# Layer 1's attention result kept once in f32 and projected by f32 products, with the work of the steps placed anew

## The chip, the core and the metric

The kernel runs on one core of a Trainium2 chip. The metric is the device time of one execution, in microseconds (us), as the median of three. A core has a matrix engine (TensorE, PE in the rows; PEld is its weight load), a vector engine (VectorE, DVE), a scalar engine (ScalarE, ACT), GpSimd (POOL), a queue engine that issues transfers (SyncE, SP) and 16 DMA engines. Each engine runs its own instructions in the order in which they are written, and the engines wait for one another by semaphores only.

## The reference, cut to what matters

Two conditioned transformer blocks act on `x` (2 x 1024 x 288), in f32. Both have 16 heads of 18 values. Block 0 is ordinary attention over tokens with an MLP behind it. In block 1 the attention runs inside a token, from head to head:

```python
# layer 1: n = 2, t = 1024, d = 288, H = 16, DH = 18
q, k, v = (qkv[:, :, 0], qkv[:, :, 1], qkv[:, :, 2])      # n t H DH
attn = jnp.einsum('nthd,ntkd->nthk', q * scale, k)        # 16 x 16 scores for each token
attn = jax.nn.softmax(attn, axis=-1)
out = jnp.einsum('nthk,ntkd->nthd', attn, v)
out = out.transpose(0, 2, 1, 3).reshape(n, t, d)          # heads first, then tokens
return out @ proj_w + proj_b
...
x = x + gate_msa[:, None, :] * _attention(...)
x = x + gate_mlp[:, None, :] * _mlp(_modulate(_layernorm(x), shift_mlp, scale_mlp), ...)
```

The `transpose` puts heads ahead of tokens before the reshape, so a row of 288 that is projected holds 16 tokens of one head. No projected tile of batch entry 0 exists before half of all steps are done, and none of entry 1 before the last step.

## The kernel before

**Precision.** Most products take a number as two f16 parts, high and low, and add the products high x high, low x high and high x low. An f32 operand goes to TensorE as it is; the trace shows two matmul records for each f32 matmul that the code issues.

**Layer 1's attention** is `head_attention`, written once for each engine. Its tokens are cut into 4 pieces of 512 (`NPIECE`), each piece into 4 steps of 128 tokens, so there are 16 steps (`NSTEP`). A step's 128 tokens make 16 "cells" of 128 x 32 numbers side by side in one PSUM bank of 128 x 512. For each step k:

- `cell_scores(k)` (PE, L1602): 16 f32 matmuls from `q_rows` and `k_ring`.
- `subtract_maxima(k)` (DVE, L1141 and L1144), `exponents_of_cells(k)` (ACT, L1379), `invert_sums(k)` (DVE, L1151 and L1154), `scale_cells(k)` (POOL, L795 and L799), `turn_cells(k)` (DVE, L1162).
- `widen(k)`: two quarters by POOL (L811), two by ACT (L1334), into `p_wide`, of which there is one buffer.
- `cell_values(k)` (PE, L1620): 16 f32 matmuls from `p_wide` and `v_cells`, into bank 6 or 7.
- `high_attention(k)` (ACT, L1384) copies the bank as f16 into `attn`; `low_attention(k)` (DVE, L1177) subtracts that from the bank and stores the rest as f16.

The loops run these staggered. In step k, PE issues the scores of k + 1 and the values of k - 2; DVE issues turn_cells(k - 2), invert_sums(k - 1), subtract_maxima(k) and, from k = 3, low_attention(k - 3); POOL issues widen(k - 2) and behind it scale_cells(k - 1).

**What else runs in the steps** is set by tables of step numbers that all engines read:

- `ROWS_AT`: `rows_mms(i, m)` (PE, L1633) makes the m-th of 7 row pieces of q, k and v of token piece i, in 7 f16 matmuls of 512 columns. `take_rows` (ACT, L1355) copies it out and stores it to `qkv_rows` in DRAM.
- SP fetches it from there: `fetch_q(i)`, `fetch_k(k)` (three buffers) and `fetch_v(i)`, which waits until all four turns of the piece before are done (`v_turned`).
- `TURN_V_AT`: `turn_v(i, a)` (DVE, L1170), four for each piece. The first step of a piece can't weigh its values before all four.
- `TILES_AT`: `normalise` and `low_part` (DVE, L936, L940 and L946) of token tiles 12 to 15, `turn` (PE, L1579) two steps later.
- `JOB_STEPS`: the MLP's weights are cut into parts: `high_weights` (ACT, L1341) one step early, `low_weights` (DVE, L1021) in the step, the next raw load (SP) two steps later. There is one raw buffer, `w_raw`.
- `OUT_AT`: `out_mms(t)` (PE, L1651) projects tile t of batch entry 0 into bank 2 or 3; `take_projection` (DVE, L1056), `add_projection` (POOL, L781) and `mid_statistics` (DVE, L926 to L931) one step later.

Behind the steps the eight tiles of batch entry 1 are projected, four, then the turns of four MLP tiles, then four. The first chunk of the MLP follows on PE (L1848).

**The projection's weights.** `attn` puts head h's value d at partition 32a + d of block r, so the 288 weight rows lie in four blocks of 128 partitions with gaps. `head_rows_job` loads them in two jobs, gaps filled with zeros; DVE splits them into `proj_high` and `proj_low` (L999 and L1008) in layer 0's last MLP chunk.

## Time and profile before

| | |
|---|---|
| time, median of 3 | 892.95 us (891.84 to 893.7) |
| the profiled execution's own time | 893.41 us |
| its span | 891.4 us |
| busy, share of the span | PE 88%, DVE 72%, ACT 59%, POOL 32% |
| layer 1's attention, from the first cell_scores to the first L1848 | 641.0 to 766.6 us |
| projections of batch entry 1 | 750.7 to 766.6 us |

The profiled execution is 0.46 us above the median. Times in the rows are from the start of the span. A busy PE is not PE at its peak, since its matmuls overlap. Where each number is read stands below, in the groups of rows.

### The profile page before, as it was taken

The page shows a single profiled execution, that of the slowest core. Times are in us where ns is not written, and L with a number is a line of the kernel's source. Part 1 is how long each engine was busy: PE and PEld are TensorE (multiplying, and loading weights), DVE is VectorE, ACT ScalarE, POOL GpSimd, SP SyncE. Part 2 cuts the span into 40 slices and gives each one's busy share as a digit, 9 for nine tenths or more (in the row PEclk, how much of TensorE's full clock was granted, in tenths as well). Part 3 has the DMA queues.
Part 4 walks back from the last instruction along what each step waited for, and adds up shares of the span by engine and source line. Part 5 has one row for each costly group of instructions (what it writes and reads, how often), then busy time and mean ns, then how long its engine had stood idle before and what let it go on. Part 6 is the DMA issues. An engine that isn't in the chain of part 4 may idle for free.

```text
span 891.4 us, 16501 instructions
## 1 busy us (share of the span) xinstructions
PE 781.1 (88%) x6096; PEld 363.8 (41%) x6096; DVE 643.1 (72%) x1277; ACT 525.9 (59%) x731; POOL 281.8 (32%) x369
## 2 busy tenths in 40 slices
PE   1569889999988989899898999999979986999996
PEld 0235222222221222222234465566646654566555
DVE  4849888898887898888936955746688897764531
ACT  4433577777776677777785725635547734634640
POOL 4311011325554241102023337241223565342122
PEclk9979799999999999999999999999989996999998
DMA  7302011110111110000040011101676730000000
GB/s 221 83 22 74 21 29 28 28 48 12 41 43 50 45 28 21 21 22 21 2 110 2 11 41 42 22 18 49 155 178 161 175 66 28 8 28 1 26 26 27
DMA packets 52127, 45.35 MB, mean 51 GB/s; under 512 B 23898, under 2 KB 41236, under 8 KB 52055
## 3 DMA queue, kind: packets, MB, share of 16 engines
q1 hardware_dynamic: 47613, 36.35, 15.9%
q10 hardware_dynamic: 4442, 8.04, 2.8%
q8 instruction: 45, 0.74, 0.4%
q14 instruction: 27, 0.22, 0.1%
HBM read 27.66 MB, written 9.46 MB: 42 GB/s over the span
## 4 chain that ended last, share of the span: by engine, by line
PE 55%; DVE 25%; ACT 5%; issue 4%; POOL 4%; DMA 3%; SPq 2%; ACTq 1%; DVEq 0%; POOLq 0%
PE ps L1869 12%; DVE row_max L966 12%; PE ps L1734 10%; PE ps L1695 8%; PE ps L1848 6%; PE ps L1633 4%; PE ps L1686 4%; PE ps L1722 3%; DVE mlp_area L1107 2%; SPq L579 2%; PE ps L1651 2%; PE ps L1602 1%; DVE probs L936 1%; DVE probs L940 1%; ACT mlp_area L1499 1%
## 5 line engine op out<-in xcount | busy, mean ns | idle before, releaser
L966 DVE TENSOR_REDUCE row_max<-ps 128x1 f32<-128x512 f32 x512 | 321.0, 684 | 55.3 <-PE ps L1695 54.2
L1458 ACT ACTIVATE probs<-ps 128x1024 f32<-128x1024 f32 x256 | 249.1, 1018 | 56.9 <-PE ps L1722 56.2
L1695 PE MATMUL ps<-stack_area 54*128 54x512 f16 x512 | 144.6, 390 | 28.3 <-DVE row_max L966 21.2
L1734 PE MATMUL ps<-probs,mlp_area 128*32 128x512 f32 x1024 | 137.2, 608 | 0.0
L1722 PE MATMUL ps<-stack_area 56*128 56x512 f16 x512 | 111.0, 385 | 7.2 <-ACT probs L1458 7.2
L1869 PE MATMUL ps<-w_fc,mlp_area 128*128 128x288 f16 x864 | 109.4, 289 | 4.7 <-DVE mlp_area L1107 4.7
L1695 PEld LDWEIGHTS ps<-stack_area 54*128 54x128 f16 x512 | 35.6, 93 | 187.2 <-DVE row_max L966 173.5
L1848 PE MATMUL ps<-mlp_area,w_fc 128*128 128x512 f16 x504 | 110.8, 379 | 0.8 <-ACT mlp_area L1499 0.8
L1499 ACT ACTIVATE mlp_area<-ps 128x512 f32<-128x512 f32 x72 | 42.9, 595 | 97.9 <-PE ps L1848 95.4
L1869 PEld LDWEIGHTS ps<-w_fc,mlp_area 128*128 128x128 f16 x864 | 84.6, 99 | 28.3 <-DVE mlp_area L1107 3.9
L769 POOL TENSOR_SCALAR neg_scaled<-neg_max 128x16 f32<-128x16 f32 x16 | 4.1, 254 | 271.2 <-DVE neg_max L973 271.2
L1848 PEld LDWEIGHTS ps<-mlp_area,w_fc 128*128 128x128 f16 x504 | 48.6, 98 | 60.7 <-ACT mlp_area L1499 4.3
L1120 DVE SCALAR_TENSOR_TENSOR probs<-ps,fc_bias 128x288 f32<-128x288 f32 x32 | 14.6, 457 | 78.1 <-PE ps L1869 78.1
L879 POOL TENSOR_TENSOR probs<-probs,ada (+2 forms) x32 | 26.1, 814 | 141.0 <-DVE probs L1120 140.7
L1107 DVE SCALAR_TENSOR_TENSOR mlp_area<-mlp_area 128x512 f16<-128x512 f32 x72 | 49.9, 701 | 17.7 <-ACT mlp_area L1503 17.5
L1503 ACT ACTIVATE mlp_area<-mlp_area 128x512 f16<-128x512 f32 x72 | 45.4, 630 | 2.7
L1722 PEld LDWEIGHTS ps<-stack_area 56*128 56x128 f16 x512 | 29.7, 94 | 36.5 <-ACT probs L1458 14.8
L1686 PE MATMUL ps<-tokens 128*126 128x512 f16 (+1 forms) x140 | 43.7, 441 | 0.0
L940 DVE SCALAR_TENSOR_TENSOR probs<-probs,rstd,ada 128x288 f32<-128x288 f32 x64 | 36.3, 567 | 8.0 <-DVE probs L936 0.9
L936 DVE SCALAR_TENSOR_TENSOR probs<-x_sb,mean_var,ada 128x288 f32<-128x288 f32 x64 | 37.0, 579 | 2.0 <-DMA ada<-ada_rows 1.0
L1579 PE MATMUL ps<-ident,probs 128*128 128x128 f16 x96 | 12.3, 270 | 28.4 <-DVE probs L946 21.8
L1633 PE MATMUL ps<-mlp_area,w_qkv 128*126 128x512 f16 (+1 forms) x147 | 35.3, 395 | 0.8 <-ACT mlp_area L1373 0.8
(170 smaller groups left out, 1082.1 us busy)
## 6 DMA issues: line engine op xcount, KB each, us to landing
stack_area<-tokens SPq DMA_DIRECT2D x124, 36.0 KB
qkv_rows<-part_area ACTq DMA_DIRECT2D x14, 252.0 KB
qkv_rows<-probs ACTq DMA_DIRECT2D x10, 252.0 KB
x_sb<-in_x SPq DMA_DIRECT2D x4, 576.0 KB, 7.6
w_raw<-in_L_cond_W_fc SPq DMA_DIRECT2D x4, 576.0 KB
tokens<-qkv_rows SPq DMA_DIRECT2D x64, 36.0 KB
v_sb<-qkv_rows SPq DMA_DIRECT2D x16, 144.0 KB
w_raw<-in_L_cond_fc_w SPq DMA_DIRECT2D x4, 576.0 KB
```

Of the source, the lines that this page charges most:

```text
L936: nc.vector.scalar_tensor_tensor(xn[u], x_sb[:, t, :], mean_var[:, t, 0:1], ada[:, b, s + 1, :], ALU.subtract, ALU.mult).then_inc(xn_done[ ...
L966: nc.vector.reduce_max(row_max[:, p % 2, t, j, half:half + 1], bank(bk), AX.X).then_inc(max_done, 1)
L1107: nc.vector.scalar_tensor_tensor(gs[:, f, 1, :], g_sb[f % 2], HS, gs[:, f, 0, :], ALU.mult, ALU.subtract).then_inc(g_split, 1)
L1458: nc.scalar.activation(probs[:, n % 2, 2 * c:2 * c + 2, :].rearrange("p h n -> p (h n)"), ps[:, 2 + 2 * c:4 + 2 * c, :].rearrange("p b n - ...
L1499: nc.scalar.activation(g_sb[f % 2], bank(2 + f % 2), gelus[l], scale=UN).then_inc(g_ready, 1)
L1633: mm = nc.tensor.matmul(bank(2 + n % 2)[0:end - first, :], w_qkv[:, w, first:end], piece_columns(i)[:, a, :], start=(x == 0), stop=(x == l ...
L1686: mm = nc.tensor.matmul(bank(bk)[0:rows], w_qk[:, w, row:row + rows], hT_all[:, a, t0:t0 + 512], start=(i == 0), stop=(i == len(PRODUCTS) ...
L1695: nc.tensor.matmul(bank(bk), stacks[rows, p % RING, 0, t * P:(t + 1) * P], stacks[rows, p % RING, 1, half * 512:(half + 1) * 512], start=T ...
L1722: mm = nc.tensor.matmul(bank(2 + 2 * c + j), stacks[rows, p % RING, 1, n * P:(n + 1) * P], stacks[rows, p % RING, 0, c * 512:(c + 1) * 512 ...
L1734: mm = nc.tensor.matmul(bank(6)[at:at + VW, :], v_pad[:, TB * (p // BPAIR) + n, 2 * (p % BPAIR) + j, :], probs[:, n % 2, 2 * c + j, :], st ...
L1848: mm = nc.tensor.matmul(bank(2 + f % 2), w_fc1[:, w, f * P:(f + 1) * P], h2T[:, a, :], start=(i == 0), stop=(i == len(PRODUCTS) - 1))
L1869: mm = nc.tensor.matmul(bank(4 + i % 2)[:, 0:C], gs[:, f, a, i * P:(i + 1) * P], w_fc2[:, w, f, :], start=(f == 0 and (a, w) == (0, 0)), s ...
```

## The change

It touches layer 1's attention alone.

- `high_attention` and `low_attention` become one copy by ACT, `take_attention`, that leaves the bank in f32. The 16 DVE subtractions are gone. PE's `cell_values` waits for the copy (`a_taken`) in place of the subtraction (`a_low`).
- The projection's weights are kept as f32 in four blocks, `proj_rows`. POOL clears them (four memsets in layer 0's second MLP chunk), SP loads 16 pieces of 18 rows and the bias straight into place (`load_heads`). The two split jobs on DVE and their raw loads are gone.
- `out_mms` issues 4 f32 matmuls of 288 columns where it issued 12 of f16.
- The tables of step numbers are new, and in a step ACT takes rows ahead of `high_weights`, widens ahead of the attention copy, and DVE splits weights ahead of `normalise`, the statistics and `take_projection`.

```diff
-        attn = [free2[:, 8192 * (1 - b):8192 * (2 - b)].bitcast(F16).rearrange("p (s r n) -> p s r n", s=2, r=4)
+        attn = [free2[:, 8192 * (1 - b):8192 * (2 - b)].bitcast(F32).rearrange("p (r n) -> p r n", r=4)
                 for b in range(B)]
-        proj_high = [w_proj_area[:, 0:2 * C], free4[:, 4608:4608 + C].bitcast(F16)]
-        proj_low = [w_proj_area[:, 2 * C:4 * C], free_v[:, 4224:4224 + C].bitcast(F16)]
+        proj_rows = [w_proj_area[:, 0:2 * C].bitcast(F32), w_proj_area[:, 2 * C:4 * C].bitcast(F32),
+                     free4[:, 4608:4608 + C], free_v[:, 4224:4224 + C]]
...
-        JOB_STEPS = {2: 5, 7: 6, 12: 7, 17: 8}
+        JOB_STEPS = {1: 3, 7: 4, 12: 5, 16: 6}
...
-        JOBS_AT_FC2 = {0: (0, 2), 3: (0, 2)}
+        JOBS_AT_FC2 = {0: (0, 2)}
...
-        TILES_AT = {2: (12, 13), 3: (14, 15)}
-        ROWS_AT = {0: [(1, 3), (1, 4)], 1: [(1, 5), (1, 6)]}
...
+        TILES_AT = {1: (12,), 2: (13, 14), 4: (15,)}
...
-        OUT_AT = {11: (0, 1), 12: (2, 3), 13: (4, 5), 14: (6,), 15: (7,)}
...
+        OUT_AT = {11: (0, 1, 2), 12: (3,), 13: (4, 5), 14: (6,), 15: (7,)}
...
+            def load_heads():
+
+                sp.wait_ge(heads_cleared, len(proj_rows))
+                rows = proj_w[1].rearrange("(r a d) n -> r a d n", r=4, a=4)
+                for r, dst in enumerate(proj_rows):
+                    for a in range(4):
+                        sp.dma_start(dst[HC * a:HC * a + D, :], rows[r, a]).then_inc(heads_in, 16)
+                sp.dma_start(proj_rows[0][D:D + 1, :], proj_b[1].rearrange("(r n) -> r n", r=1)).then_inc(heads_in, 16)
...
-            load_weights(1, QKV_JOBS, HEAD_JOBS)
+            load_heads()
...
-            def low_attention(k):
-
-                b, dst = k // 8, attn_cells(k // 8, 1, k)
-                dve.wait_ge(a_high, k + 1)
-                nc.vector.tensor_tensor(dst, bank(6 + k % 2).rearrange("p (x t g) -> p x t g", t=2, g=4), attn_cells(b, 0, k),
-                                        ALU.subtract).then_inc(a_low, 1)
...
-            def high_attention(k):
+            def take_attention(k):
 
                 act.wait_ge(ev_mm, k + 1)
-                nc.scalar.activation(attn_cells(k // 8, 0, k), bank(6 + k % 2).rearrange("p (x t g) -> p x t g", t=2, g=4), ACT.Copy
-                                     ).then_inc(a_high, 1)
+                nc.scalar.activation(attn_cells(k // 8, k), bank(6 + k % 2).rearrange("p (x t g) -> p x t g", t=2, g=4), ACT.Copy
+                                     ).then_inc(a_taken, 1)
...
                 if k > 1:
-                    pe.wait_ge(a_low, k - 1)
+                    pe.wait_ge(a_taken, k - 1)
...
-                steps = [(r, s, part) for r in range(4) for s, part in ((0, proj_high), (1, proj_high), (0, proj_low))]
-                for x, (r, s, part) in enumerate(steps):
-                    mm = nc.tensor.matmul(bank(2 + t % 2)[:, 0:C], attn[b][:, s, r, cols],
-                                          part[r // 2][:, C * (r % 2):C * (r % 2 + 1)],
-                                          start=(x == 0), stop=(x == len(steps) - 1))
+                for r in range(4):
+                    mm = nc.tensor.matmul(bank(2 + t % 2)[:, 0:C], attn[b][:, r, cols], proj_rows[r],
+                                          start=(r == 0), stop=(r == 3))
```

The rest of the tables, as piece and number by step: the row pieces were (1,3) (1,4) in step 0, (1,5) (1,6) in 1, three of piece 2 in step 3 and two each in 4 and 5, three of piece 3 in step 6 and two each in 7 and 8. They are (1,3) to (1,6) in step 0, three of piece 2 in step 2, two in 3, one in 5 and one in 6, of piece 3 one in step 6, four in 7, one each in 8 and 9. The turns of v were four in step 0, then two each in 3, 4, 8, 9, 12 and 13; they are four in step 2, one each in 4 and 5, two each in 6, 8, 9, 12 and 13.

What stands in a row on DVE in steps 1 and 2, first before. L1151 opens invert_sums, L1141 subtract_maxima, L1162 is turn_cells, L1021 the weight split, L936 and L940 a tile's normalise.

```order
L1170 STREAM_TRANSPOSE v_sb<-v_sb 128x512 [waits v_in] x4
L1151 TENSOR_REDUCE v_sb<-probs 128x32 [waits cell_exp]
L1154 RECIPROCAL v_sb<-v_sb 128x32 [waits cell_total]
L1141 TENSOR_REDUCE v_sb<-ps 128x32 [waits cell_sub,cell_mm]
L1144 TENSOR_TENSOR part_area<-ps,v_sb 128x512 [waits cell_top]
L1162 STREAM_TRANSPOSE stack_area<-probs 128x512 [waits cell_done]
L1151 TENSOR_REDUCE v_sb<-part_area 128x32 [waits cell_exp]
```

The same place in the changed kernel (L1143, L1133, L1154 and L1013 are these lines there, L928 and L932 normalise, L938 low_part, L1162 turn_v):

```order
L1136 TENSOR_TENSOR part_area<-ps,v_sb 128x512 [waits cell_top]
L1013 SCALAR_TENSOR_TENSOR w_fc<-w_raw,w_fc 128x1152 [waits late_high]
L928 SCALAR_TENSOR_TENSOR probs<-x_sb,mean_var,ada 128x288
L932 SCALAR_TENSOR_TENSOR probs<-probs,rstd,ada 128x288 [waits xn_done0,rstd_ready]
L1154 STREAM_TRANSPOSE stack_area<-probs 128x512 [waits cell_done]
L1143 TENSOR_REDUCE v_sb<-part_area 128x32 [waits cell_exp]
L1146 RECIPROCAL v_sb<-v_sb 128x32 [waits cell_total]
L1133 TENSOR_REDUCE v_sb<-ps 128x32 [waits cell_sub,cell_mm]
L1136 TENSOR_TENSOR probs<-ps,v_sb 128x512 [waits cell_top]
L938 TENSOR_TENSOR probs<-probs 128x288 [waits hi_ready0]
```

Two normalise pairs and the four turns of v follow there, as the last work of step 2; before, the turns were the last of step 0. The split of the weights and a normalise moved ahead of the first turn_cells.

PE in step 11 before, with two projections ahead of the scores of step 12:

```order
L1651 MATMUL ps<-w_proj,mlp_area 128x288 [waits a_low,rows_taken,w_ready]
L1651 MATMUL ps<-w_proj,mlp_area 128x288 x5
L1651 MATMUL ps<-stack_area,mlp_area 128x288 x2
L1651 MATMUL ps<-v_sb,mlp_area 128x288
L1651 MATMUL ps<-stack_area,mlp_area 128x288 x2
L1651 MATMUL ps<-v_sb,mlp_area 128x288
```

And in the changed kernel, where the third tile's first matmul waits for DVE to have taken the first (`proj_y`), and the scores (L1585) stand behind it:

```order
L1633 MATMUL ps<-w_proj,mlp_area 128x288 [waits a_taken,rows_taken,heads_in]
L1633 MATMUL ps<-w_proj,mlp_area 128x288
L1633 MATMUL ps<-stack_area,mlp_area 128x288
L1633 MATMUL ps<-v_sb,mlp_area 128x288
L1633 MATMUL ps<-w_proj,mlp_area 128x288 [waits rows_taken]
L1633 MATMUL ps<-w_proj,mlp_area 128x288
L1633 MATMUL ps<-stack_area,mlp_area 128x288
L1633 MATMUL ps<-v_sb,mlp_area 128x288
L1633 MATMUL ps<-w_proj,mlp_area 128x288 [waits proj_y]
```

A tile went from 12 matmuls to 4, and three tiles stand in step 11 instead of two.

## Rows read from the trace of the kernel before

**Rows 1.** Two stretches: us; busy us (records) of PE, PEld, DVE, ACT, POOL; clock; DMA

```profile
680.00:700.00 20.00, 20.00 (x249) 12.82 (x246) 12.93 (x21) 14.73 (x24) 7.29 (x13) 1.00 0.68 169
720.00:740.00 20.00, 15.28 (x264) 10.56 (x255) 19.61 (x37) 6.98 (x12) 14.21 (x21) 1.00 0.12 33
```

**Rows 2.** The chain that ended last, 749 to 767 us: start, us, what

```profile
749.23 0.61 ACT mlp_area L1384
749.86 0.70 DVE mlp_area L1177
750.70 8.17 PE ps L1651 x48
...
760.76 5.99 PE ps L1651 x48
```

**Rows 3.** A stretch of the first four projections, TensorE alone: busy, clock

```profile
752.00:754.00 2.00, 2.00 (x10) 0.50 0.00 0
```

**Rows 4.** f32 on TensorE by line: ns min/median/max, first and last start, shapes

```profile
L1744 PE MATMUL ps<-w_fc,silu_t x24: 406/406/431, 63.1 to 64.4; 96*32 96x288 f32 x24
L1710 PEld LDWEIGHTS ps<-ident,w_qkv x64: 138/140/144, 124.2 to 477.0; 128*128 128x128 f32 x64
```

**Rows 5.** TensorE in order of time: start, us, line, shapes [idle before, releaser]

```profile
122.92 1.06 PE L1734 MATMUL ps<-probs,mlp_area 128*32 128x512 f32 x8
...
661.12 1.95 PE L1602 MATMUL ps<-tokens,stack_area 128*32 128x128 f32 x32 [3.22 <-DMA tokens<-qkv_rows]
662.99 6.38 PE L1633 MATMUL ps<-mlp_area,w_qkv 128*126 128x512 f16 x21
...
685.87 4.75 PE L1633 MATMUL ps<-mlp_area,w_qkv 128*126 128x512 f16 x21
```

**Rows 6.** VectorE in step 15, in order of time: start, us, line

```profile
736.64 0.70 DVE L1162 STREAM_TRANSPOSE stack_area<-part_area 128x512 f32<-128x512 f32 x1
...
739.49 0.45 DVE L1056 SCALAR_TENSOR_TENSOR probs<-ps,ada 128x288 f32<-128x288 f32 x1
739.85 0.68 DVE L1177 TENSOR_TENSOR mlp_area<-ps,mlp_area 128x512 f16<-128x512 f32 x1
740.45 0.70 DVE L1162 STREAM_TRANSPOSE stack_area<-probs 128x512 f32<-128x512 f32 x1
```

**Rows 7.** VectorE: the L1162 that open steps 11, 12, 13, 14, 17, and two statistics

```profile
710.27 0.71 DVE L1162 STREAM_TRANSPOSE stack_area<-part_area 128x512 f32<-128x512 f32 x1
...
714.47 0.70 DVE L1162 STREAM_TRANSPOSE stack_area<-probs 128x512 f32<-128x512 f32 x1
...
717.32 0.45 DVE L926 BATCH_NORM_STATS2 bn<-x_sb 128x6 f32<-128x288 f32 x1
...
718.10 0.45 DVE L926 BATCH_NORM_STATS2 bn<-x_sb 128x6 f32<-128x288 f32 x1
...
725.08 0.66 DVE L1162 STREAM_TRANSPOSE stack_area<-part_area 128x512 f32<-128x512 f32 x1
...
732.86 0.68 DVE L1162 STREAM_TRANSPOSE stack_area<-probs 128x512 f32<-128x512 f32 x1
...
744.10 0.71 DVE L1162 STREAM_TRANSPOSE stack_area<-part_area 128x512 f32<-128x512 f32 x1 [1.45 <-POOL part_area L799]
```

**Rows 8.** GpSimd in order of time: the widen of step 10, the last widen

```profile
707.44 1.27 POOL L811 COPY stack_area<-stack_area 32x512 f32<-32x512 f32 x2 [1.04 <-DVE stack_area L1162]
...
744.87 2.31 POOL L811 COPY stack_area<-stack_area 32x512 f32<-32x512 f32 x2 [0.81 <-DVE stack_area L1162]
```

**Rows 9.** ScalarE's first high_weights of the steps

```profile
652.29 1.16 ACT L1341 ACTIVATE w_fc<-w_raw 128x1152 f16<-128x1152 f32 x1 [0.86 <-DMA w_raw<-in_L_cond_fc_w]
```

**Rows 10.** VectorE: the first four turns of v, a normalise, the first weight split

```profile
644.60 3.93 DVE L1170 STREAM_TRANSPOSE v_sb<-v_sb 128x512 f32<-128x512 f32 x4 [0.20 <-DMA v_sb<-qkv_rows]
...
655.40 0.51 DVE L936 SCALAR_TENSOR_TENSOR probs<-x_sb,mean_var,ada 128x288 f32<-128x288 f32 x1
...
656.46 1.35 DVE L1021 SCALAR_TENSOR_TENSOR w_fc<-w_raw,w_fc 128x1152 f16<-128x1152 f32 x1
```

74 lines of the change are left out of this document (29 added, 45 removed).

## Prediction

> **What bounds the kernel now.** I read the stretches first, to see which engine is full where the change acts [rows 1], then the chain of waits behind the steps [rows 2], then each engine in order of time inside the steps [rows 5 to 8]. There are three parts. From about 662 to 703 us TensorE is full (20.00 of 20 us) and the vector engine is not (12.93): the row pieces fill it. From about 703 to 741 us it is the other way round, DVE 19.61 of 20 and PE 15.28. From 747 us on the chain of waits shows what is last [rows 2]: last values, ACT's copy, DVE's subtraction, and then TensorE without a gap through eight projections and four turns to the MLP at 766.6 us. So a vector instruction saved counts in the second part only, and a TensorE instruction added counts in the first and third.
>
> **The product, priced.** Four f16 projections take 5.99 us in 48 matmuls [rows 2], 1.50 us a tile. No row shows an f32 matmul of 128 rows and 128 weight columns that isn't a transpose. The nearest are of 32 weight columns, four side by side. Eight of 512 columns take 1.06 us [rows 5]: two groups, so at most 0.53 us for 512 columns and 0.30 for 288, with the last one's tail in it. The 24 of 288 columns start within 1.3 us [rows 4], six groups, five steps, 0.26. As an estimate, 0.24 to 0.26 us a record, two records for each matmul issued, eight a tile: 1.95 us. That is 0.45 us more than now, for every one of the 16 tiles. The bounds: 1.9 (0.24) and 2.1 (0.26); 0.30 holds a tail that a stream hides. A 128-column f32 weight load takes 0.138 us [rows 4], and lies under a 0.24 us matmul if it overlaps as the f16 loads do.
>
> **Last part: eight tiles.** 8 x 0.45 = +3.6 us (bounds 3.2 and 4.8), all on the path, since TensorE has no gap there. The first four tiles took 8.17 us where the others took 5.99, at half the clock [rows 2, 3], a loss of 2.2. TensorE idles between the last value products as before, so I keep this loss; it can come out 1 less or 1.5 more, for a slower stream that starts at another moment.
>
> **First part: the start.** The early row pieces move ahead. TensorE idled 3.22 us before the scores at 661.12, waiting for a fetch [rows 5]; three pieces in step 2 can fill that. But the turns of v of piece 0 moved from step 0 to the end of step 2, and the first values wait for them. The vector engine can't come there early: `low_weights` now stands in step 1, and its `high_weights` can't begin before the raw weights land at 652.3 and takes 1.16 [rows 9]. From 653.5 on DVE has in a row: split 1.3 [rows 10], a normalise 1.06 (656.46 - 655.40 [rows 10]), one step of turn, sums and maxima 2.85 (739.49 - 736.64 [rows 6]), a low part of some 0.4, two normalises 2.1, four turns 3.9 [rows 10]. That ends near 665.1. Until then TensorE can do the scores of step 3 and three row pieces; then it idles some 3 us. By the same moment the kernel before had done 0.7 of a piece, one step's scores (1.75) and one step's values (1.0) more: the change is 2.3 pieces of 1.58 us (4.75 / 3 [rows 5]) ahead and 2.75 behind, 0.9 ahead. In step 4, which has no row piece, ACT's two column copies stand ahead of its widen, and the values wait about 1.1 us. The clock fell before in the like idle time (21 row matmuls took 6.38 us where 21 others took 4.75 [rows 5]), and some 0.6 us of that loss came behind 665; I take 0.8. Sum at the values of step 9: -0.9 + 1.1 + 0.2 = +0.4. Bounds -3 (the 3.22 us of idle filled at no price) and +3 (it comes back in full). `fetch_v(1)` now waits for the turns, and holds fetch_k(6), fetch_k(7) and a weight load behind it on SP's queue; I expect them in time, by some 3 us.
>
> **Second part: steps 9 to 13.** Each low_attention takes 0.60 us to the next instruction [rows 6]. But a step has a second limit. turn_cells, widen (1.27), mask, scale and their waits go round between DVE and GpSimd: from the widen's start at 707.44 to the next turn at 710.27 is 2.83, with the turn ahead and its wait (0.74) 3.57 [rows 7, 8]. A bare step with the subtraction takes 3.8 (740.45 - 736.64, with a take) [rows 6]. So bare steps gain 0.25, not 0.60. In detail: steps 9 and 10 give 0.8 by the start of step 11 (710.3 to 709.5), where TensorE arrives last. Step 11 took 4.20 [rows 7]. Now three tiles stand ahead of the scores: 3 x 1.95 from 709.5 is 715.4, and the take of the third and the next turn come at 716.0: 6.5 us. Step 12 took 10.61 [rows 7]; less 0.60, less one take 0.36 [rows 6], plus one statistic 0.78 [rows 7], less some waits, 10.3. Step 13 took 7.78; less 0.60, less one statistic: 6.4. Step 14 begins at 709.5 + 6.5 + 10.3 + 6.4 = 732.7, now 732.86: -0.2. The projections of this part thus eat the vector engine's gain, mostly in step 11.
>
> **Steps 14 to 17 and the last values.** Now 732.86 to 744.10, 11.24 us [rows 7]. By the round trip 3 x 3.57 = 10.7. The last weight split moves from step 17 to 16. Beside it GpSimd's last widen took 2.31 us for 1.27 [rows 8]; now this 1.04 falls on step 16's widen or scale, and no longer on the last widen. So the turn of step 17 comes at 732.7 + 10.7 + 1.0 = 744.4, +0.3; the widen behind it gives back 1.04, and the subtraction that goes, 749.86 to 750.70, gives 0.84 [rows 2]. The first projection starts at 750.7 + 0.3 - 1.0 - 0.8 = 749.2, -1.5 to -1.7.
>
> The row shows a loss of 1.04 beside a split of 1.3. The Trainium skill (SBUF — State Buffer, the part on the shared port pair) says that VectorE with two SBUF inputs and GpSimd exclude each other for a whole instruction. By it the price could be the split's full length, 1.3, in step 16, and the total 0.3 higher than by the row.
>
> **At no price.** The two split jobs in layer 0's last chunk: DVE waits there for row pieces and ACT anyway. POOL's four memsets of 288 columns: GpSimd, busy 32% of the span, waits for DVE behind them in that chunk; without that cover, each would cost what a copy of 512 columns does, 0.6 us [rows 8]. `load_heads` issues 17 transfers early, for 18 in two bursts. ACT's copy keeps its length; only the output's type differs.
>
> **Sum.** Start of the last projections -1.6, eight tiles +3.6, clock 0: +2.0 us. On the profiled execution's 893.4 this is 895.4; it stands 0.46 above the median of the runs, so 892.95 + 2.0 = 895.0.
>
> **The rivals.**
> 1. *The vector engine's gain carries (faster).* If TensorE reaches step 11 early enough that the third projection doesn't hold the scores, and the start keeps its lead, ten subtractions in steps 9 to 18 come off in full, 6.0 us. Then 892.95 - 6.0 + 3.6 = 890.5. For it: TensorE was busy 15.28 of 20 us there [rows 1], and the eight tiles add only 3.6. Against: the round trip of 3.57, and three tiles in a row. It decides from 2.5 us of lead at step 11.
> 2. *Gain and price balance.* The early pieces keep 2 us of their lead, nothing else differs: 893.0.
> 3. *The clock.* Half clock for two more tiles' length in the last part, or a second fall in step 2 or 4: +2 to +3, 897.5. For it: new idle near 662 and 675 us. A page speaks for it too: the Trainium skill (TensorE: Matmul & The Clock Gate, on loop structure) warns that idle gaps halve the clock.
> 4. *Weight loads don't overlap.* Each f32 record would cost 0.24 + 0.138 [rows 4], 64 of them in the last part +8.8, more in the steps: 904. Against it: at 0.125 us an f16 record hides a load of 0.10. The Trainium skill (TensorE: Matmul & The Clock Gate, the mechanism of packing) states that loads overlap a running matmul only if the row group differs. By that rule this rival is what happens; the f16 rows speak against it.
> 5. *The change doesn't do what it says:* the spread row pieces win nothing since the values wait for the turns of v. That is in my forecast.
>
> **How the numbers follow.** Forecast 0.45 (its own range 893.6 to 897), rival 1 0.22, rival 2 0.20, rival 3 0.09, rival 4 0.04. A measurement of this kernel tells about 0.2%, 1.8 us, from no change. The forecast lies just beyond that, so some 0.1 of its 0.45 falls within; rival 2 lies within. Faster 0.23, same 0.31, slower 0.46. The range for 8 in 10 runs from rival 1's 890.5, its far side left out, to 898.3 in rival 3.
>
> **What would show it.** Right: the f32 projection at about 0.24 us a record; the last part, first projection to first L1848's like, at 19 to 20 us against 15.9; the first values near 665 us, released by DVE's turns of v; in step 11 the vector engine waiting 2 us for projections; the last projections starting near 749. Wrong: a start of the last part before 747 (rival 1), a tile of 3 us (rival 4), TensorE's clock at half for over 5 us in the last part (rival 3).

## The result, and the profile after

The changed kernel takes 896.0 us (median of 9 runs, 894.6 to 897.1), the kernel before 892.6 (9 runs beside it). The ratio is 1.004, with a 95% interval of 1.0027 to 1.0053: 3.4 us slower. That is the forecast's side and inside its range; the forecast was 895.0.

The profiled executions have spans of 891.4 and 893.7 us, 2.3 apart. I cut both at four marks: the first matmul of layer 0's last MLP chunk (591.99 before, 591.09 after), the first `cell_scores` matmul, the first projection behind the steps, and the MLP's first matmul of layer 1. The 0.9 us ahead of the first mark is there already at 498 us (an MLP chunk starts at 498.88 before and 497.99 after), ahead of the first instruction that the change adds, GpSimd's memsets at 547.4. So the change itself is 3.2 us here, near the 3.4 of the runs.

| from mark to mark, us | before | after | difference |
|---|---|---|---|
| to the first scores | 49.01 | 48.64 | -0.37 |
| first scores to first projection behind the steps | 109.70 | 108.84 | -0.86 |
| last part: eight tiles, four turns | 15.88 | 20.23 | +4.35 |
| MLP to the end | 124.82 | 124.90 | +0.08 |

The chain that ended last, from the last part of the steps on (start, us, what); L801 is GpSimd's widen, L1603 the values, L1367 ACT's copy, L1633 the projection, L1562 and L1565 the turns, L1829 the MLP. It answers to [rows 2].

```profile
744.18 0.80 POOL stack_area L801
744.98 0.06 issue
745.04 0.74 POOL stack_area L801
745.78 0.04 issue
745.82 1.98 PE ps L1603 x32
747.80 0.02 issue
747.82 0.61 ACT mlp_area L1367
748.43 0.14 issue
748.57 10.55 PE ps L1633 x32
...
761.01 7.96 PE ps L1633 x32
```

The subtraction is gone from it, and the projections hold 10.55 and 7.96 us where they held 8.17 and 5.99 [rows 2].

The f32 product itself, by line: ns min/median/max, first and last start, shapes. It answers to [rows 4].

```profile
L1633 PEld LDWEIGHTS ps<-w_proj,mlp_area x64: 186/190/337, 707.9 to 767.4; 128*128 128x128 f32 x64
L1633 PE MATMUL ps<-w_proj,mlp_area x64: 406/406/819, 707.9 to 767.6; 128*128 128x288 f32 x64
```

A record's 0.406 us is its length with its tail; the next one starts 0.242 us later (two records of a name start to start, 0.48 in the order of time). A tile has four matmuls of two records each, eight in all: 1.94 us.

The stretches of after (us; busy us of PE, PEld, DVE, ACT, POOL; clock; DMA share, GB/s), which answer to [rows 1]:

```profile
680.00:700.00 20.00, 20.00 (x255) 12.43 (x257) 15.18 (x23) 14.62 (x24) 8.48 (x12) 1.00 0.64 159
700.00:720.00 20.00, 20.00 (x283) 14.20 (x287) 16.43 (x28) 12.20 (x19) 12.40 (x19) 1.00 0.63 136
720.00:740.00 20.00, 17.13 (x244) 12.04 (x236) 18.61 (x43) 8.98 (x14) 15.07 (x24) 1.00 0.10 31
740.00:760.00 20.00, 15.31 (x113) 11.23 (x114) 10.09 (x19) 5.92 (x12) 7.65 (x9) 0.66 0.10 30
```

TensorE is now full from 680 to 720 us, not to 703 only, and VectorE, which held 703 to 741 before, has time to spare there (16.43 of 20). In the last stretch the clock is again at half for a part.

Waits of the steps, in order of time (start, us, engine, line, what, [idle before, releaser]); L1162 turns v, L1154 opens a step, L1048 takes a projected tile:

```profile
664.00 1.08 PE L1603 MATMUL ps<-stack_area,v_sb 128*32 128x128 f32 x32 [2.38 <-DVE v_sb L1162]
...
714.28 0.46 DVE L1048 SCALAR_TENSOR_TENSOR probs<-ps,ada 128x288 f32<-128x288 f32 x1 [1.70 <-PE ps L1633]
```

Both were foretold: the first values wait for the turns of v, and VectorE waits in step 11 for the third f32 tile.

### The profile page after: what moved, and what is told of

Its sections match the earlier page's. It is cut to its first block, busy times and chain, and to the rows that moved or that the text cites. A ratio compares the mean times of both kernels' runs of the same rounds, so it can differ in the third digit from the quotient of the medians.

```text
span 893.7 us, 16353 instructions
## 1 busy us (share of the span) xinstructions
PE 788.5 (88%) x6032; PEld 369.5 (41%) x6032; DVE 631.6 (71%) x1257; ACT 526.8 (59%) x731; POOL 284.0 (32%) x373
## 4 chain that ended last, share of the span: by engine, by line
PE 58%; DVE 23%; ACT 5%; POOL 5%; issue 4%; SPq 2%; DMA 2%; ACTq 1%; DVEq 0%; POOLq 0%
PE ps L1850 12%; DVE row_max L958 12%; PE ps L1715 10%; PE ps L1676 8%; PE ps L1829 6%; PE ps L1616 4%; PE ps L1667 4%; PE ps L1703 3%; PE ps L1633 3%; DVE mlp_area L1099 2%; PE ps L1585 2%; SPq L569 2%; ACT mlp_area L1482 1%; DVE probs L928 1%; PE ps L1603 1%
## 5 line engine op out<-in xcount | busy, mean ns | idle before, releaser
L1829 PE MATMUL ps<-mlp_area,w_fc 128*128 128x512 f16 x504 | 110.9, 379 | 0.8 <-ACT mlp_area L1482 0.8
L1829 PEld LDWEIGHTS ps<-mlp_area,w_fc 128*128 128x128 f16 x504 | 48.5, 98 | 61.0 <-ACT mlp_area L1482 4.5
L932 DVE SCALAR_TENSOR_TENSOR probs<-probs,rstd,ada 128x288 f32<-128x288 f32 x64 | 37.0, 579 | 8.0 <-DVE probs L928 0.9
L928 DVE SCALAR_TENSOR_TENSOR probs<-x_sb,mean_var,ada 128x288 f32<-128x288 f32 x64 | 36.4, 569 | 2.3 <-DMA ada<-ada_rows 1.4
L1562 PE MATMUL ps<-ident,probs 128*128 128x128 f16 x96 | 11.9, 262 | 27.9 <-DVE probs L938 23.0
```

The lines of the kernel that those rows point to most:

```text
L1829: mm = nc.tensor.matmul(bank(2 + f % 2), w_fc1[:, w, f * P:(f + 1) * P], h2T[:, a, :], start=(i == 0), stop=(i == len(PRODUCTS) - 1))
```

## The experiments

All stand beside runs of the kernel before on the same chip. "Marks" below are, in the profiled execution: from the first scores to the first projection behind the steps, and the length of the last part. Of the ratio stands the 95% interval.

| kernel | median | ratio to before | steps | last part |
|---|---|---|---|---|
| before | 892.6 | 1 | 109.70 | 15.88 |
| after | 896.0 | 1.0027 to 1.0053 | 108.84 | 20.23 |
| e1_cols216 | 891.7 | 0.9996 to 1.0026 | 109.32 | 16.19 |
| e2_old_places | 894.2 | 1.0007 to 1.0045 | 109.03 | 20.42 |
| e3_new_places | 898.6 | 1.0068 to 1.0109 | 115.76 | 16.11 |
| e4_no_low | 889.4 | 0.9964 to 0.9992 | 107.44 | 15.34 |
| e5_split17 | 896.9 | 1.0030 to 1.0061 | 109.34 | 19.79 |
| e6_two_out | 893.2 | 0.9992 to 1.0027 | 107.46 | 19.49 |
| e7_turns0 | 891.9 | 0.9967 to 1.0002 | 106.07 | 20.16 |
| e8_late_out | 889.6 | 0.9951 to 0.9979 | 106.16 | 17.68 |
| e9_late_out_f16 | 888.1 | 0.9929 to 0.9966 | 105.05 | 16.39 |
| e10_late_turns0 | 887.0 | 0.9924 to 0.9964 | 103.38 | 17.68 |
| e11_f16_early_norm | 886.2 | 0.9920 to 0.9951 | 106.78 | 14.15 |
| e12_f16_table | 887.4 | 0.9931 to 0.9963 | 104.82 | 15.66 |

My theory: the f32 product's price in the last eight tiles makes the loss, and what VectorE saves doesn't reach the end because TensorE or the round with GpSimd is last in the steps. The rivals: the loss lies in the new places (three tiles in step 11, turns of v behind three row pieces), or in the clock.

A mark is read from one execution of each kernel, so its spread has to be known. After, e1, e5, e6 and e8 have the same code up to step 11, and the turn that opens it came 68.95, 69.48, 69.88, 69.31 and 68.99 us behind the first scores: 0.9 us between equal code. After has the least of them. From there on, after and e1, with the same code to the last projections, need 39.88 and 39.84 us. So a difference behind step 11 is read from its opening, and one of under 1 us ahead of it is not taken for the edit's. The profiled executions of e2 (898.3) and e9 (883.7) were the slowest and the fastest of their runs.

### The price of the last eight tiles

```diff
-                    mm = nc.tensor.matmul(bank(2 + t % 2)[:, 0:C], attn[b][:, r, cols], proj_rows[r],
+                    wide = C if t < TB else 216
+                    mm = nc.tensor.matmul(bank(2 + t % 2)[:, 0:wide], attn[b][:, r, cols], proj_rows[r][:, 0:wide],
```

> The changed kernel, with the matmuls of the last eight projected tiles (those behind the steps) over 216 of their 288 columns; it leaves out the last 72 columns of layer 1's projection for batch entry 1. A record of 288 columns took 0.242 us, so one of 216 should take 0.182 (or 0.19, the length of its weight load) and a tile 1.46 to 1.52 us, what a tile of twelve f16 matmuls took before. Theory 1, the eight tiles behind the steps carry the loss: the last part, first of these projections to the MLP's first matmul, falls from 20.2 to 16.3 us, and the whole kernel is 3.9 us faster than the changed one, at 0.999 to 1.001 of the kernel before. Theory 2, the loss lies in the steps (two or three long tiles ahead of the scores, the row pieces' new places): the last part falls likewise, but only if it isn't at half clock for longer; then the kernel would stay 1.5 us or more above the one before. Theory 3, the f32 weight loads bind and not the columns: a tile stays at 1.9 us, and the time of the changed kernel doesn't move.

The last part took 16.19 us, 4.04 less than after, and the kernel measures as the one before (1.0011; the interval leaves room for up to 2.3 us above it). With the tiles of the last part at the old price no loss can be told; theory 1. Theory 3 is out: with a quarter fewer columns the records start every 0.18 us and no longer every 0.242, so the 190 ns loads don't bind.

### The other half of the change: where things stand

e2 puts all tables and both orders of the steps back and keeps the f32 product; e3 moves them in the kernel before and keeps its f16 parts. The main lines of e3 (e2 is their reverse in the changed kernel):

```diff
-        JOB_STEPS = {2: 5, 7: 6, 12: 7, 17: 8}
+        JOB_STEPS = {1: 5, 7: 6, 12: 7, 16: 8}
-        TILES_AT = {2: (12, 13), 3: (14, 15)}
+        TILES_AT = {1: (12,), 2: (13, 14), 4: (15,)}
-        OUT_AT = {11: (0, 1), 12: (2, 3), 13: (4, 5), 14: (6,), 15: (7,)}
+        OUT_AT = {11: (0, 1, 2), 12: (3,), 13: (4, 5), 14: (6,), 15: (7,)}
...
-                    if k > 2:
-                        high_attention(k - 3)
                     for t in TILES_AT.get(k - 1, ()):
                         high_part(0, t % 2, NT + t, 2)
                     if 1 < k < NSTEP + 2:
                         widen(k - 2)
+                    if k > 2:
+                        high_attention(k - 3)
```

with `ROWS_AT` and `TURN_V_AT` as in the change.

> The changed kernel's f32 copy and f32 projection, but row pieces, turns of v, tiles, projections and weight splits at the steps, and in the order within a step, where the kernel before has them. Computes everything. Theory 1 (the prediction's sum: at the front the new places gain nothing, and in steps 11 to 13 they only move projections): within 1 us of the changed kernel, 895 to 897 on its scale. Theory 2, the new places are needed to make room for the f32 tiles: 2 us or more slower than the changed kernel, 898 or more. Theory 3, the new places cost (turns of v behind three row pieces, three tiles in step 11, a split beside step 16's widen): 1.5 us or more faster than the changed kernel, 894.5 or less, with the last projections starting at least 1.5 us earlier.

> The other half: the kernel before with its f16 parts and its twelve matmuls a tile, but with row pieces, turns of v, tiles, projections and weight splits at the steps of the changed kernel, and in its order within a step. Computes everything. Theory 1 (places worth little by themselves): 892 to 893.5 against 892.6 of the kernel before. Theory 2 (the new places win where the tiles are short, since three f16 tiles in step 11 cost 4.5 us and not 5.9): 890 to 891.5, ratio 0.997 to 0.999. Theory 3 (they cost, and the f32 copy's saved subtractions hid it): 894 or more, ratio above 1.0015.

e2's last projections start 0.19 us later than after's: the f32 kernel has almost nothing from the new places, at least nothing that one execution of each tells. Its median is 1.9 us below after's, but against other runs, and the intervals of the two ratios overlap. Theory 2 is out. The median, 894.2, is theory 3's, but the sign that theory 3 named, last projections 1.5 us earlier, isn't there, as theory 1 said; the two stay undecided.

e3 is theory 3, and by more than it said: the same places cost the f16 kernel 6.06 us. Its trace shows how in step 8, which takes 10.2 us for 8.0 in after (VectorE, L1172 is the subtraction, L1379 ACT's copy; then ACT, L1350 takes row pieces):

```profile
695.92 0.69 DVE L1139 TENSOR_TENSOR probs<-ps,v_sb 128x512 f32<-128x512 f32 x1
701.24 0.69 DVE L1172 TENSOR_TENSOR mlp_area<-ps,mlp_area 128x512 f16<-128x512 f32 x1 [4.62 <-ACT mlp_area L1379]
701.85 2.09 DVE L1165 STREAM_TRANSPOSE v_sb<-v_sb 128x512 f32<-128x512 f32 x2
```

```profile
697.63 1.22 ACT L1350 ACTIVATE part_area<-ps 62x512 f32<-62x512 f32 x2 [0.77 <-PE ps L1628]
698.88 0.32 ACTq L1362 DMA_DIRECT2D qkv_rows<-part_area  x1
699.29 1.29 ACT L1329 ACTIVATE stack_area<-stack_area 32x512 f32<-32x512 f32 x2 [0.45 <-ACT part_area L1350]
700.61 0.60 ACT L1379 ACTIVATE mlp_area<-ps 128x512 f16<-128x512 f32 x1
```

The subtraction waits for ACT's copy, the copy stands behind four row pieces and the widen, and behind the subtraction VectorE's queue holds the turns of v and the next turn of cells. The copy comes late in the changed kernel too, but there no subtraction waits on VectorE for it. So the two halves need each other: the f32 half (no subtraction, but longer tiles) is worth 115.76 - 108.84 = 6.9 us at the new places, and only 109.70 - 109.03 = 0.7 at the old.

### VectorE's saving alone

```diff
-                    if k > 2:
-                        low_attention(k - 3)
...
-                    pe.wait_ge(a_low, k - 1)
+                    pe.wait_ge(a_high, k - 1)
...
-                    mm = nc.tensor.matmul(bank(2 + t % 2)[:, 0:C], attn[b][:, s, r, cols],
+                    mm = nc.tensor.matmul(bank(2 + t % 2)[:, 0:C], attn[b][:, 0, r, cols],
```

> The kernel before without the sixteen subtractions that form the low part of the attention result; the matmuls of the low part read the high part in its place, so that their number and length stay. It leaves out what the low part adds to layer 1's projection. It prices VectorE's saving by itself. By the prediction's steps: 0.8 us by the start of step 11, up to 0.6 each in steps 11, 12 and 13, 0.25 in each of the steps 14 to 17, 0.84 behind the last values: 4 us in all, 888.5, with the last projections starting near 746.7 (against 750.7). Rival A, the whole vector saving counts (sixteen by 0.6): 883. Rival B, the round between VectorE and GpSimd sets the steps, and TensorE step 11: only the last 0.84 and little else, 891 to 892.

The start of the last projections moved 2.26 us, the medians 2.6 (2.0 by the ratio); forecast 4, so it lies between that and rival B. The turns that open the steps, from the first scores, tell where (us):

| | step 11 | 12 | 13 | 14 | 17 | last projections |
|---|---|---|---|---|---|---|
| before | 69.27 | 73.47 | 84.08 | 91.86 | 103.10 | 109.70 |
| e4_no_low | 69.50 | 73.09 | 83.27 | 90.41 | 101.44 | 107.44 |
| e2_old_places | 69.92 | 73.82 | 84.90 | 91.98 | 103.02 | 109.03 |
| after | 68.95 | 74.93 | 85.09 | 91.39 | 103.67 | 108.84 |
| e6_two_out | 69.31 | 73.12 | 82.90 | 90.01 | 102.30 | 107.46 |
| e7_turns0 | 66.22 | 72.20 | 82.35 | 88.64 | 100.91 | 106.07 |
| e8_late_out | 68.99 | 72.60 | 80.98 | 86.91 | 101.11 | 106.16 |

Up to step 11, eight subtractions gave nothing that shows: 69.50 for 69.27. Against e4 0.45 had come up by step 6 (40.65 for 40.20), so from there they gave 0.2. TensorE has no gap there until 704 us, and step 10, the one bare step behind, is 3.57 us long before and 3.60 in e4, the round between VectorE and GpSimd of the prediction. Steps 11, 12 and 13 gave 0.61, 0.43 and 0.64, steps 14 to 16 0.22 together, and the last 0.6 came behind the turn of step 17. The f32 tiles then take 1.2 of it back: e2, which has both, ends its steps at 109.03 to e4's 107.44; 0.4 of the 1.6 stands ahead of step 11, where there is no tile yet, and 1.2 in steps 11 and 12, where VectorE waits for TensorE to finish the second and the fourth tile (0.22 and 0.75 us).

### The weight split and the last widen

```diff
-        JOB_STEPS = {1: 3, 7: 4, 12: 5, 16: 6}
+        JOB_STEPS = {1: 3, 7: 4, 12: 5, 17: 6}
```

> The changed kernel with its last weight split back in step 17, where it stands beside GpSimd's last widen and no longer beside step 16's (2.51 us there, 1.25 above an undisturbed one). Computes everything. Theory 1, the price only changes its place: the turn of step 17 comes 1.0 to 1.2 us earlier, the last widen takes about 1 us longer, and the first of the last projections starts within 0.3 us of where it did, counted from the first scores (108.8). Theory 2, step 16 has room for it and step 17 none: the last projections start 1 us later, and the kernel is 1 us slower. Theory 3, step 16 is the dearer place, since mask and scale come behind the widen there: 0.5 to 1 us faster than the changed kernel.

Theory 1 in kind: from the opening of step 11 the turn of step 17 comes 1.27 us earlier than in after, and the last widen is 0.84 longer. The first of the last projections started 0.50 later from the first scores, where 0.3 at most was foretold, but 0.93 of lateness stood before step 11; from there it starts 0.4 earlier. GpSimd's widens in order of time, of after and then of this kernel (steps 16 and 17):

```profile
739.34 2.51 POOL L801 COPY stack_area<-stack_area 32x512 f32<-32x512 f32 x2
...
744.18 1.59 POOL L801 COPY stack_area<-stack_area 32x512 f32<-32x512 f32 x2 [0.81 <-DVE stack_area L1154]
```

```profile
742.57 1.26 POOL L801 COPY stack_area<-stack_area 32x512 f32<-32x512 f32 x2
...
746.17 2.43 POOL L801 COPY stack_area<-stack_area 32x512 f32<-32x512 f32 x2 [0.81 <-DVE stack_area L1154]
```

The price of 1.25 us moves from one widen to the other, and the times can't be told apart (1.004 and 1.0046). The 1.59 of after's last widen lies beside VectorE's normalises (744.04 to 746.7), 0.33 above the bare 1.26.

### Three tiles in step 11

```diff
-        OUT_AT = {11: (0, 1, 2), 12: (3,), 13: (4, 5), 14: (6,), 15: (7,)}
+        OUT_AT = {11: (0, 1), 12: (2, 3), 13: (4, 5), 14: (6,), 15: (7,)}
```

> The changed kernel with two projected tiles in step 11 and two in step 12, as the kernel before has them, in place of three and one. Computes everything. Theory 1, the third 1.95 us tile ahead of the scores of step 12 costs VectorE the 1.70 us that it waits there: step 11 falls from 5.98 to about 4.3 us, step 12 grows by its own take and statistic (0.8) at most, and the last projections start 1 us earlier from the first scores than 108.84. Theory 2, the third tile only moves the wait from step 11 to step 12: no change within 0.3 us.

Theory 1, and more than it said: step 11 fell from 5.98 to 3.81 us, steps 12 and 13 took 9.78 and 7.11 for 10.16 and 6.30, and the last projections start 1.38 us earlier, 1.7 counted from the opening of step 11. The third tile cost the change 1.4 to 1.7 us.

### The turns of v

```diff
-        TURN_V_AT = {2: [(0, 0), (0, 1), (0, 2), (0, 3)], 4: [(1, 0)], ...
+        TURN_V_AT = {0: [(0, 0), (0, 1), (0, 2), (0, 3)], 4: [(1, 0)], ...
```

> The changed kernel with the four turns of the first v piece back in step 0, row pieces and all else as in the changed one. Computes everything. It tests the prediction's term for the front. Theory 1, the turns hold TensorE: the 2.38 us that it idled before the first values (released by VectorE) go, and since TensorE is full from there to step 12 the lead lasts: the turn that opens step 11 comes 1.5 to 2.4 us earlier from the first scores (68.95 before), the kernel is 1 to 2 us faster than the changed one. Theory 2, a part comes back as a wait for transfers and in step 11: 0 to 0.7 us. Theory 3, the scores of step 2 come late for it: slower by 1 us or more.

Theory 1. TensorE goes from three row pieces to the values without a gap, where after waited 2.38 us:

```profile
656.20 6.17 PE L1616 MATMUL ps<-mlp_area,w_qkv 128*126 128x512 f16 x21
662.30 1.08 PE L1603 MATMUL ps<-stack_area,v_sb 128*32 128x128 f32 x32
```

Step 11 opens 2.73 us earlier than in after, and the last projections start 2.77 earlier: the lead passes through every later step whole. Against e1, e5 and e6, which share after's code up to there, the lead is 3.1 to 3.7. The runs fell by more than foretold, from 1.004 to 0.9985 of the kernel before, some 5 us; what of that is neither the lead nor spread, no trace shows. With the turns there the f32 kernel is level with the kernel before (0.9967 to 1.0002).

### Later tiles, and both

```diff
-        OUT_AT = {11: (0, 1, 2), 12: (3,), 13: (4, 5), 14: (6,), 15: (7,)}
+        OUT_AT = {11: (0,), 12: (1,), 13: (2,), 14: (3,), 15: (4,), 16: (5, 6), 17: (7,)}
```

e10 has this and e7's line.

> The changed kernel with the eight tiles of the steps projected later: one each in steps 11 to 15, two in 16, one in 17 (before: three in 11, one in 12, two in 13, one in 14 and 15). Computes everything. Theory 1, TensorE and VectorE are full up to step 13 and wait in steps 14 to 17: the work fits into those waits. VectorE's 1.70 us of waiting in step 11 goes, 1 us or so of takes moves to where it waits, the last projections start 1.5 to 3 us earlier from the first scores, and with less idle TensorE loses less to the clock in the last part (2.55 us before): 2 to 5 us faster than the changed kernel, so at or below the kernel before. Theory 2, the late tiles stand in the round between VectorE and GpSimd (the 1.95 us tiles ahead of scores or of the last values, GpSimd's additions): 1 to 3 us slower. Theory 3, three tiles in step 11 cost nothing in the end: no change.

> The changed kernel with its first four turns of v in step 0 and its eight tiles of the steps projected late (steps 11 to 17) together. Each by itself brought the start of the last projections forward, by 2.8 and by 2.7 us from the first scores; the late tiles also kept TensorE at full clock in the last part, 2.55 us. Computes everything. Theory 1, the two are separate (the one at the front, the other behind step 11) and add: last projections 103.4 us after the first scores, last part 17.7 us, 886.5 to 887.5 in all, 8 us or more below the changed kernel. Theory 2, with the lead of the front, the steps from 11 on are held by the round between VectorE and GpSimd and part of the gain is lost: 888 to 889.

Theory 1 for both. e8 starts the last projections 2.68 us earlier, e10 5.46. That the two gains add to 5.45, so near it, is partly luck, as the spread ahead of step 11 is 0.9 us. Both have a last part of 17.68 us, 2.55 less than after: what after lost to the clock there. Another 1.2 to 1.3 us of both lies in the MLP behind, which no edit touches (see the last section). The idle of TensorE ahead of the last values, in after and in e8:

```profile
741.90 1.94 PE L1603 MATMUL ps<-stack_area,tokens 128*32 128x128 f32 x32 [3.82 <-POOL stack_area L801]
745.82 1.94 PE L1603 MATMUL ps<-stack_area,tokens 128*32 128x128 f32 x32 [1.98 <-POOL stack_area L801]
748.57 2.26 PE L1633 MATMUL ps<-w_proj,mlp_area 128*128 128x288 f32 x4 [0.81 <-ACT mlp_area L1367]
```

```profile
740.40 1.08 PE L1603 MATMUL ps<-stack_area,tokens 128*32 128x128 f32 x32 [0.66 <-POOL stack_area L801]
745.07 1.08 PE L1603 MATMUL ps<-stack_area,tokens 128*32 128x128 f32 x32 [1.45 <-POOL stack_area L801]
746.96 1.21 PE L1633 MATMUL ps<-w_proj,mlp_area 128*128 128x288 f32 x4 [0.81 <-ACT mlp_area L1367]
```

and the stretch of e8, at full clock where after had 0.66:

```profile
740.00:760.00 20.00, 17.34 (x149) 13.04 (x150) 10.45 (x23) 7.89 (x13) 9.46 (x13) 1.00 0.11 30
```

Tiles that lay ahead of the scores, where VectorE had to wait for them, now lie in the waits of steps 14 to 17. TensorE's waits there are shorter, and the granted clock didn't fall, in e8 and in e10 alike.

### The same for the kernel before

e12 has only the table; e9 also multiplies the low part last in the first tile and splits the weights behind the subtraction of step 17; e11 also changes VectorE's order in the last part.

```diff
-        OUT_AT = {11: (0, 1), 12: (2, 3), 13: (4, 5), 14: (6,), 15: (7,)}
+        OUT_AT = {11: (0,), 12: (1,), 13: (2,), 15: (3,), 16: (4, 5), 17: (6, 7)}
...   (e9, e11)
+                steps = [(r, 0, part) for r in range(4) for part in (proj_high, proj_low)]
+                steps += [(r, 1, proj_high) for r in range(4)]
...
+                    if t % TB == 0 and x == 8:
+                        pe.wait_ge(a_low, 8 * (b + 1))
...   (e11)
+                    if k == NSTEP + 2:
+                        dve.wait_ge(cell_wide, 2 * NSTEP)
+                        dve.wait_ge(late_wide, 2 * NSTEP)
+                        mlp_normalise(1, 0, 0)
```

> The kernel before with only the table of its eight tiles changed (one each in steps 11, 12, 13, 15, two in 16, two in 17); the weight split and the low part stay where they were. Computes everything. It tells what of the late f16 version's 4.65 us (last projections from the first scores: 109.70 to 105.05) is the table's. Theory 1, the table carries most: 3 us earlier there, and the last part at full clock with the takes' waits, 889 to 890. Theory 2, the split and the low part carry it: 1.5 us or less from the table, 890.5 to 892.

> The kernel before, changed in three places by what the traces show: its eight tiles of the steps go later (one each in steps 11, 12, 13, 15, two in 16, two in 17); the last weight split stands behind the subtraction of step 17, after the last widen's start; and the first of the last eight tiles multiplies the low part last, so that the last subtraction lies beside eight matmuls. Computes everything. Theory 1, all three lie on the path: 0.7 us for the subtraction, 0.5 to 1.0 for the widen, 1 for the takes, up to 2 for the clock of the last part, in all 2.5 to 4.5 us faster than the kernel before, 888 to 890. Theory 2, only the subtraction and the widen count: 1 to 1.5 us, 891. Theory 3, the late tiles push the scores or the values and eat it: no gain, or slower.

> The late f16 version (late tiles, split behind the subtraction, low part multiplied last) with VectorE's work of the last part in another order: the first MLP normalise stands between the last widen and the last subtraction, where VectorE waited 2.9 us, and each tile's sum is taken before the next normalise. Computes everything. In the run before it TensorE waited 1.80 and 0.48 us for these takes at full clock. Theory 1, they go: the last part falls from 16.4 to 14.2 us, 2 us faster than that version, 886. Theory 2, VectorE has 7 us of work ahead of the four turns in any order, and the wait comes back at the turns: gain 1 us or less. Theory 3, the normalise delays the last subtraction or shares its time with the widen: slower.

e12: theory 1, and more; its steps end 4.88 us earlier, and the kernel is faster by 0.4 to 0.7%. Of the 4.88 the table can have only what comes from step 11 on, where it begins to differ: 36.85 us for 40.44, 3.6. In the profile a further 1.7 us lies in the MLP behind. The clock fell in the steps instead of ahead of the last part: 0.83 in 720 to 740 us, in e9 and e11 too, where before has 1.00. e9 adds nothing that the runs show (0.9947 both). Its last subtraction is off the path, but its last projections start 0.23 us later than e12's and its last part is 0.73 longer. The first is the split again: moved ahead of the takes, it stands beside GpSimd's `invert` (L737), which comes ahead of the last widen (GpSimd, e12 and then e9):

```profile
740.88 0.55 POOL L737 TENSOR_TENSOR rstd<-mean_var,power 128x1 f32<-128x1 f32 x1
```

```profile
737.24 1.66 POOL L737 TENSOR_TENSOR rstd<-mean_var,power 128x1 f32<-128x1 f32 x1
739.11 1.27 POOL L811 COPY stack_area<-stack_area 32x512 f32<-32x512 f32 x2 [0.21 <-issue]
```

The second is VectorE's takes, behind its normalises (TensorE, in order of time, e9 and then e11):

```profile
747.22 0.66 PE L1658 MATMUL ps<-w_proj,mlp_area 128*128 128x288 f16 x4 [1.80 <-DVE probs L1056]
749.35 0.66 PE L1658 MATMUL ps<-w_proj,mlp_area 128*128 128x288 f16 x4 [0.48 <-DVE probs L1056]
```

```profile
751.68 0.66 PE L1660 MATMUL ps<-w_proj,mlp_area 128*128 128x288 f16 x4 [0.22 <-DVE probs L1056]
```

With the other order e11's last part is 14.15 us, 2.24 less, as its theory 1 said. Its steps ended 1.7 us later than e9's, and all of that stands before step 11, in code that both share. In the runs the two can't be told apart: 0.9935 against 0.9947, within each other's intervals. e11 and e10 are the fastest of each kind, 0.4 to 0.8% below the kernel before, and can't be told apart either.

## Why the prediction was right, and where not

**Last eight tiles, +3.6.** Right in kind and cause (e1), and a little small: 20.23 - 15.88 = +4.35. Two terms were mis-sized. The record came out at 0.242 us, the low end of the estimate. But I read 1.50 us a tile before from a group of 5.99, which holds the tail of its last record. From the first record of the second four tiles to the MLP's first, before took 766.58 - 760.69 = 5.89 and after 768.80 - 760.94 = 7.86: 0.49 us a tile more, 3.9 in all. The other 0.4 is the clock's. It came back to full near 755.0 us before and 753.7 after, as the stretch shows in which it changed, of before and then of after (clock 0.96 and 0.63):

```profile
755.00:756.00 1.00, 1.00 (x9) 0.81 (x8) 0.90 (x2) 0.00 (x0) 0.90 (x1) 0.96 0.00 0
```

```profile
753.00:754.00 1.00, 1.00 (x4) 0.79 (x3) 0.90 (x3) 0.00 (x0) 0.61 (x1) 0.63 0.00 0
```

The projections began at 750.70 and 748.57, so they ran 4.4 us at half clock before and 5.2 after, and lost half of that: 2.2 and 2.6. By the same count the last parts of e6 and e7 (3.7 and 5.0 us at half clock) should be 1.8 and 2.5 longer than e8's 17.68, 19.5 and 20.2; they are 19.49 and 20.16. The record is not what grew, the stretch is: "a slower stream that starts at another moment" had the sign, and I priced it at nothing. Rival 3 in small.

**Weight loads, rival 4.** Out. A load took 0.190 us and not 0.138, but records start every 0.242 us, so it lies under the matmul. The Trainium skill (TensorE: Matmul & The Clock Gate, mechanism of packing) says that loads overlap only if the row group differs; here all loads and matmuls are of 128 rows, and they overlap. The measurement decides against that sentence as I used it. The same section also lets a load run ahead into a background weight buffer, and with that the measurement agrees.

**The front, +0.4.** Values of step 9 came at 64.59 us from the first scores, for 64.50. In the four other executions of the same code they came at 64.6 to 65.5, so +0.4 was right as far as that spread tells, and so was its mechanism: 2.38 us of idle, released by the turns of v, near 664, and 0.89 ahead of the values of step 4 (1.1 foretold). e7 shows what the place of the turns is worth, 2.77.

**Steps 9 and 10, -0.8.** Wrong. From the values of step 9 to the turn that opens step 11 before takes 4.76 us and after 4.37, as in all its executions: 0.4 gained. e2, without the subtraction but at the old places, takes 4.81, so the 0.4 is the places'; in e4, which isolates the saving, it is 0.2. The step that failed is "steps 9 and 10 give 0.8 by the start of step 11, where TensorE arrives last": up to 704 us TensorE is full, and step 10 has the length of the round trip with or without the subtraction (3.57 and 3.60). Both limits stood in my own text, and I took the gain all the same. The sum also lost its own term there: with +0.4 at the values of step 9 and -0.8 behind, step 11 opens at 709.9 and not at 709.5.

**Steps 11, 12, 13.** 6.5, 10.3, 6.4 foretold; 5.98, 10.16 and 6.30 measured, with the 1.70 us wait for the third tile (2 foretold). Step 14 opened 0.47 earlier (-0.2 foretold). e6 shows what the third tile cost in the end, 1.4 to 1.7 us.

**Steps 14 to 17.** The turn of step 17 came 0.57 later (+0.3 foretold). The widen beside the split lost 1.25 us, not the 1.04 of [rows 8]. By the rule of the Trainium skill (SBUF — State Buffer, shared port pair) it would be the split's full 1.29: the rule was nearer than the row. The row had its widen begin 0.14 us after the split, and in after the split begins 0.75 behind the widen. The last widen then gave back 0.72 and not 1.04; VectorE, free of the subtraction, ran ahead into the normalises beside it, which no run separates.

**First projection, -1.6.** Measured -0.86 (-0.38 in e1's execution of the same code). Against the forecast, 0.5 us was missing at the opening of step 11, 0.8 came back in steps 11 to 13, 0.6 was lost in steps 14 to 16 and 0.4 behind them. So the number is nearer than its parts, which is luck.

**At no price: the split jobs of layer 0.** Wrong by 0.37, in the change's favour. TensorE waited 0.84 us there before (at 634.7, for ACT) and 0.47 after, and all of e1, e2 and after show 48.64 or 48.65 to the first scores, where before, e3 and e4 show 49.01, 49.00 and 48.99. GpSimd's four memsets took 0.33 us each, not 0.6, and cost nothing: from the chunk's start at 498 us to the first mark it is 93.1 us in both.

**Sum.** -0.37 - 0.86 + 4.35 + 0.08 = +3.2, for +2.0 foretold. The f32 tiles are its price; that the steps gave back only 0.9 is the tables' doing, since e6 and e7 each bring the same f32 kernel level with the one before.

**Rival 1** was nearer than I made it. I said that it decides from 2.5 us of lead at step 11, when the third tile no longer holds the scores. e7 has a lead of 2.73 over after, and step 11 is as long as in after (5.98), so that mechanism isn't what happens; the lead passes whole all the same. No threshold was to be seen.

## What to carry to other kernels

Work saved on one engine counts only from the point where that engine is last; run the edit alone (e4) before trusting a count of instructions times duration, and look at what stands behind each wait in its queue (e3). When an engine idles near the end of a stage, move independent work of the full stretch there (e8, e12: 2.7 and 3.6 us), which in e8 and e10 also kept TensorE's clock up. Read a group's length start to start, not with its tail, when you turn it into a price per piece. And look at how far marks differ between executions of equal code before you read an edit from them.

## What the hardware showed that I had not expected

A wait of TensorE cost it the clock in one execution and not in the next. Two stretches of before and of e12, which have the same code there and the same busy time in the first:

```profile
658.00:662.00 4.00, 0.89 (x16) 0.73 (x20) 3.93 (x8) 3.09 (x6) 2.51 (x4) 0.69 0.63 134
662.00:666.00 4.00, 4.00 (x27) 2.17 (x20) 2.46 (x5) 0.00 (x0) 0.00 (x0) 0.50 0.62 129
```

```profile
658.00:662.00 4.00, 0.87 (x16) 0.66 (x20) 3.93 (x8) 2.85 (x6) 2.50 (x4) 1.00 0.61 128
662.00:666.00 4.00, 4.00 (x34) 2.41 (x27) 2.11 (x5) 0.60 (x1) 0.00 (x0) 1.00 0.61 136
```

Before is at half clock (1.2 GHz) behind the wait, e12 at full (2.4 GHz), and e12's step 6 opens 1.1 us earlier (39.10 to 40.20 from the first scores). That can be a part of why runs of one kernel spread over several microseconds, the kernel before from 887.1 to 893.5 in one series; and 1.1 of e12's 4.88 is this and not its table.

The last 125 us show it again. They took 123.1 to 123.8 in e5 and e8 to e12 and 124.8 to 125.4 in all others. TensorE's last group of matmuls there, in before and in e12:

```profile
870.25 15.07 PE L1869 MATMUL ps<-w_fc,mlp_area 128*128 128x288 f16 x108 [2.08 <-DVE mlp_area L1107]
```

```profile
864.89 13.40 PE L1869 MATMUL ps<-w_fc,mlp_area 128*128 128x288 f16 x108 [2.08 <-DVE mlp_area L1107]
```

The work and the wait of 2.08 us ahead of it are the same. In before the clock was at half in 872 to 874 us, in e12 at full throughout. In 860 to 880 us it reads 0.91 in all eight profiles that took the longer time and 1.00 in all six that took the shorter. So the clock is the 1.7 us; e5, which has it at full, differs from after by one entry of a table and isn't faster in its runs. What makes the clock fall behind this wait in one execution and not in another stays open, and 1.2 to 1.7 us of what e8 to e12 gain in their profiles is this.
